# An attention and mixture-of-experts kernel: the filling of expert rows moved into the attention, and three smaller changes of order

## The reference

```
x = x + attn_a(layernorm(x))   # 16 heads, latent 32, rotary embedding, causal softmax
x = x + ffn(layernorm(x))      # 8 experts, 128 -> 512 -> 128, exact gelu; each token goes to its top 2
x = x + attn_b(layernorm(x))   # 16 heads of 8, causal softmax
x = x + ffn(layernorm(x))      # the same expert weights again
```

## Time and profile before

| what | value |
|---|---|
| median of 3 runs (1228.84 to 1236.98) | 1233.25 us |
| profiled execution: its time, its span | 1235.08 us, 1233.3 us |
| PE busy | 1038.6 us, 84% |
| DVE busy | 860.1 us, 70% |
| GpSimd busy | 734.7 us, 60% |
| ACT busy | 656.8 us, 53% |
| mean granted TensorE clock | 0.918 |
| chain that ended last | PE 50%, DVE 25%, issue 8%, SPq 7%, DMA 4%, POOL 3% |

### The profile page before, as it was taken

One profiled execution on the slowest core, in us unless ns is written; L12 is line 12 of the kernel. 1 busy time (PEld: TensorE's weight loads), 2 busy tenths in 40 slices (PEclk: granted clock), 3 DMA queues, 4 the chain that ended last, 5 costly groups with the idle time before them and its releaser, 6 DMA issues.

```text
span 1233.3 us, 31859 instructions
## 1 busy us (share of the span) xinstructions
PE 1038.6 (84%) x11223; PEld 779.5 (63%) x11224; DVE 860.1 (70%) x2217; ACT 656.8 (53%) x1205; POOL 734.7 (60%) x809
## 2 busy tenths in 40 slices
PE   4689999988888988449988888999999974499995
PEld 3466666666665656239988745666666642398995
DVE  4697889888789997525565577677777764255665
ACT  1266776656465655115544556777777741154552
POOL 0476776767667777715544424667878866155553
PEclk9699999889699999769999989999999987599998
DMA  5340000000000000222333200000000002223335
GB/s 118 82 87 3 2 2 2 11 10 10 8 10 12 11 10 19 74 55 72 96 93 92 82 18 1 2 2 10 15 17 14 19 20 70 52 76 98 101 104 147
DMA packets 69358, 53.27 MB, mean 43 GB/s; under 512 B 20770, under 2 KB 61346, under 8 KB 69218
## 3 DMA queue, kind: packets, MB, share of 16 engines
q1 hardware_dynamic: 56578, 29.78, 9.6%
q0 software_dynamic: 9088, 18.70, 4.6%
q10 hardware_dynamic: 3552, 2.95, 1.0%
HBM read 27.57 MB, written 23.81 MB: 42 GB/s over the span
## 4 chain that ended last, share of the span: by engine, by line
PE 50%; DVE 25%; issue 8%; SPq 7%; DMA 4%; POOL 3%; ACT 2%; DVEq 0%; POOLq 0%; ACTq 0%
PE PS L1851 7%; PE PS L1533 5%; PE PS L1612 5%; PE PS L1663 4%; PE PS L1535 4%; PE PS L1534 4%; PE PS L1594 3%; DMA xg<-expert_in 3%; DVE M L1004 3%; DVE swapped L1032 2%; DVE M L996 2%; PE PS L1601 2%; SPq L582 2%; PE PS L1643 2%; DVE swapped L1030 2%
## 5 line engine op out<-in xcount | busy, mean ns | idle before, releaser
L1310 ACT ACTIVATE PT<-PS 128x768 f32<-128x768 f32 x256 | 206.7, 808 | 118.0 <-PE PS L1680 69.9
L754 POOL DMA_INDIRECT expert_out<-y_rows,dest x156 | 151.9, 974 | 194.8 <-DVE y_rows L1224 170.3
L643 POOL TENSOR_SCALAR_AFFINE_SELECT PT<-PT 128x512 f32<-128x512 f32 x256 | 185.7, 726 | 85.2 <-ACT PT L1310 84.4
L1446 ACT ACTIVATE hid<-PS,b_cols 128x256 f32<-128x256 f32 x312 | 122.2, 474 | 93.9 <-PE PS L1535 93.9
L1851 PE MATMUL PS<-W,hid 128*128 x1248 | 152.3, 275 | 0.2
L660 POOL DMA_INDIRECT expert_in<-rows,slots x128 | 130.0, 1015 | 29.6 <-issue 25.0
L1851 PEld LDWEIGHTS PS<-W,hid 128*128 128x128 f32 x1248 | 146.2, 192 | 0.5 <-issue 0.5
L1612 PE MATMUL PS<-PT,v_aug 128*32 128x256 f32 (+1 forms) x2048 | 115.1, 345 | 2.5 <-POOL PT L643 2.5
L1594 PE MATMUL PS<-causal_b,ident_b 128*128 128x256 bf16 x512 | 103.8, 287 | 8.2 <-DVE q_aug L1096 7.2
L1533 PE MATMUL PS<-xg_hi,w_hi 128*128 128x256 f32 x312 | 96.4, 309 | 2.3 <-DVE xg_lo L1203 1.7
L683 POOL TENSOR_TENSOR straight<-whole,C 128x512 f32<-128x512 f32 x64 | 82.8, 1293 | 21.0 <-ACT whole L1329 19.9
(11 more groups left out here) (292 smaller groups left out, 3159.9 us busy)
## 6 DMA issues: line engine op xcount, KB each, us to landing
xg<-expert_in SPq DMA_DIRECT2D x78, 129.0 KB
got<-expert_out SPq DMA_DIRECT2D x64, 128.0 KB
expert_out<-y_rows,dest POOLq DMA_INDIRECT x156
W<-in_L_ffn_w_dram SPq DMA_DIRECT2D x1, 2048.0 KB, 10.4
expert_in<-rows,slots POOLq DMA_INDIRECT x128
expert_in<-C SPq DMA_DIRECT2D x16, 128.0 KB
out_dram<-X SPq DMA_DIRECT2D x8, 256.0 KB
b_rows<-in_L_ffn_b_dram SPq DMA_DIRECT2D x2, 512.0 KB
```

The costliest lines, as they stand in the source:

```text
L643: nc.gpsimd.affine_select(out=diagonal, in_=diagonal, pattern=[[0, 4], [1, P]], compare_op=ALU.is_ge, fill=0.0, base=0, channel_multiplier ...
L754: nc.gpsimd.indirect_dma_start(out=expert_out, out_offset=bass.IndirectOffsetOnAxis(ap=dest[:, i % 4, b_:b_ + 1], axis=0), in_=y_rows[:, i ...
L1310: s.activation(PT[:, unit % 2, 2 * pair:2 * pair + 2, 0:3 * P], PS[:, 4:6, 0:3 * P], ACT.Exp).then_inc(m["exp_done"], 1)
L1446: ins = s.activation(hid[:, r % 2, k, :], h_bank[r % 2][k // 2][:, k % 2 * ROWS:(k % 2 + 1) * ROWS], ACT.Gelu, bias=b1_cols[:, bass.ds(e * ...
```

## The change

It has four parts. `KNOWN` is chunk 4. Right after chunk 4 is ranked, DVE copies its counts to `end_of` and raises `ends_ready`; SP then fills, behind each expert's end as it stands after chunk 4, SAFE = 3 x 512 + 256 = 1792 rows, where before it filled 256 rows behind the final end. The rows come first and the single numbers second. GpSimd waits for `filled` ahead of chunk 5's sends, since these write into the filled rows. ACT's wait on `ends_ready` ahead of the experts becomes one on `attended`. SP loads the results of token tile i - 16 in slot i. In `LAST` the last output product (`out_t`, `out`) stands ahead of chunk 6's gate, and the buffers of the statistics are exchanged to suit. In attention a GpSimd's unit becomes: end the rope of the unit before, mask pair 1 of the unit before, mask pair 0, start this unit's rope, send, root.

```diff
+KNOWN = NCH - 4
+SAFE = (NCH - 1 - KNOWN) * CH + ROWS
...
-    LAST = [("rank", 0, -2, 4), ("turn", 1, 0, 7), ("gate_t", 0, -1, 0), ("gate", 0, -1, 1), ("out_t", 0, 0, 2), ("out", 0, 0, 3), ("rank", 0, -1, 4),
+    LAST = [("rank", 0, -2, 4), ("turn", 1, 0, 7), ("out_t", 0, 0, 2), ("out", 0, 0, 3), ("gate_t", 0, -1, 0), ("gate", 0, -1, 1), ("rank", 0, -1, 4),
             ("gate_t", 0, 0, 7), ("gate", 0, 0, 0), ("rank", 0, 0, 1)]
...
-                sp.wait_ge(attended[n], 1)
-                sp.dma_start(b2_rows[:, :, :].rearrange("p e d -> p (e d)"), b2.rearrange("e d -> (e d)").partition_broadcast(P)).then_inc(me["bias_ready"], 16)
-
                 sp.wait_ge(me["ends_ready"], 1)
                 with nc.allow_non_contiguous_dma(reason="one number in each row"):
                     for e in range(E):
-                        end = sp.value_load(end_of[0:1, e:e + 1], min_val=0, max_val=E * STRIDE - ROWS)
-                        sp.dma_start(expert_in[bass.ds(end, ROWS), D:WIDE].rearrange("(j p) w -> p j w", p=P),
-                                     con("aside")[:, e * RB:(e + 1) * RB].unsqueeze(2)).then_inc(me["filled"], 16)
-                        sp.dma_start(expert_in[bass.ds(end, ROWS), 0:D].rearrange("(j p) w -> p j w", p=P),
-                                     ident.unsqueeze(1).broadcast_to([P, RB, D])).then_inc(me["filled"], 16)
+                        end = sp.value_load(end_of[0:1, e:e + 1], min_val=0, max_val=E * STRIDE - SAFE)
+                        sp.dma_start(expert_in[bass.ds(end, SAFE), 0:D].rearrange("(j p) w -> p j w", p=P),
+                                     ident.unsqueeze(1).broadcast_to([P, SAFE // P, D])).then_inc(me["filled"], 16)
+                        sp.dma_start(expert_in[bass.ds(end, SAFE), D:WIDE].rearrange("(j p) w -> p j w", p=P),
+                                     con("aside")[:, e * SAFE // P:(e + 1) * SAFE // P].unsqueeze(2)).then_inc(me["filled"], 16)
+
+                sp.wait_ge(attended[n], 1)
+                sp.dma_start(b2_rows[:, :, :].rearrange("p e d -> p (e d)"), b2.rearrange("e d -> (e d)").partition_broadcast(P)).then_inc(me["bias_ready"], 16)
...
                     load(i, r, least)
-                    if least >= LAG:
-                        load_results(i - LAG, (least - LAG) % CT, least - LAG)
+                    if least > LAG:
+                        load_results(i - LAG - 1, (least - LAG - 1) % CT, least - LAG - 1)
...
                     if k == 0:
                         pool.wait_ge(m["targets_ready"], c + 1)
+                        if c == KNOWN + 1:
+
+                            pool.wait_ge(moe_sems["1" if n == "a" else "2"]["filled"], 16 * 2 * E)
...
                     if unit and plan.project[unit - 1]:
                         end_rope(plan.project[unit - 1])
+                    if unit:
+                        mask(m, unit - 1, 1)
                     mask(m, unit, 0)
+                    if plan.project[unit]:
+                        start_rope(plan.project[unit])
                     if sends_at(unit, FIRST_SENT["a"]):
                         chunk, k = sends_at(unit, FIRST_SENT["a"])
                         send("a", chunk, range(k, k + 1))
-                    if plan.project[unit]:
-                        start_rope(plan.project[unit])
-                    mask(m, unit, 1)
                     if statistics_a(unit) is not None:
                         root(m, normal_a(unit + 1)[1])
-                last_sends("a", m, 0)
+                mask(m, NCH * UNITS - 1, 1)
+                last_sends("a", m, 1)
...
+            def known_ends(m, me, s):
+
+
+                if s.c == KNOWN:
+                    dve.wait_ge(m["freed_dve"], s.freed)
+                    v.tensor_copy(end_of[:, :], counts[0:1, KNOWN, :]).then_inc(me["ends_ready"], 1)
+
```

More of the change, by code:

```diff
@@ L42 @@
 _at = 0
-for _name, _n in (("ident", P), ("cos", S), ("sin", S), ("tile_no", TILES), ("ids", 2 * CT), ("aside", (2 * E - 1) * RB), ("first_row", E), ("prefer", E), ("steps", 6), ("place", 1),
+for _name, _n in (("ident", P), ("cos", S), ("sin", S), ("tile_no", TILES), ("ids", 2 * CT), ("aside", (E * SAFE + SPARE) // P), ("first_row", E), ("prefer", E), ("steps", 6), ("place", 1),
                   ("stack", 2), ("one24", 1),
@@ L78, in constants @@
     put("ids", 2 * (p[:, None] + P * (np.arange(2 * CT) // 2)) + np.arange(2 * CT) % 2)
-    put("aside", 2 * T + p[:, None] + P * np.arange((2 * E - 1) * RB))
+    put("aside", 2 * T + p[:, None] + P * np.arange((E * SAFE + SPARE) // P))
     put("first_row", np.broadcast_to(STRIDE * np.arange(E, dtype=np.float32), (P, E)))
@@ L215 @@
     FIRST_LATE = [("key", 2, 0), ("key", 3, 0), ("prep", 0, 1), ("key", 0, 1), ("key", 1, 1), ("key", 2, 1), ("key", 3, 1), ("prep", 0, 2)]
-    LAST = [("rank", 0, -2, 4), ("turn", 1, 0, 7), ("gate_t", 0, -1, 0), ("out_t", 0, 0, 1), ("gate", 0, -1, 2), ("out", 0, 0, 3), ("rank", 0, -1, 4),
+    LAST = [("rank", 0, -2, 4), ("turn", 1, 0, 7), ("out_t", 0, 0, 1), ("out", 0, 0, 3), ("gate_t", 0, -1, 0), ("gate", 0, -1, 2), ("rank", 0, -1, 4),
             ("gate_t", 0, 0, 7), ("gate", 0, 0, 0), ("rank", 0, 0, 1)]
@@ L332, in program @@
     expert_in = nc.dram_tensor("expert_in", [E * STRIDE + SPARE, WIDE], F32, kind="Internal").ap()
-    expert_out = nc.dram_tensor("expert_out", [2 * T + E * ROWS + SPARE, D], F32, kind="Internal").ap()
+    expert_out = nc.dram_tensor("expert_out", [2 * T + E * SAFE + SPARE, D], F32, kind="Internal").ap()
     result_tiles = expert_out[0:2 * T, :].rearrange("(t p k) d -> p t (k d)", p=P, k=2)
@@ L395, in program @@
         table_i = sb("table_i", [1, 5, TILES], I32)
+        end_of = sb("end_of", [1, E], I32)
         v_aug = sb("v_aug", [P, 2, CT, H, L])
@@ L457, in program @@
             table_f = sb("table_f", [P, 5], F32, moe)
-            end_of = sb("end_of", [1, E], I32, moe)
         used = [0, 0]
@@ L558, in _ @@
             with nc.allow_non_contiguous_dma(reason="one number in each row"):
-                sp.dma_start(expert_in[E * STRIDE:, D:WIDE].rearrange("(j p) w -> p j w", p=P), con("aside")[:, E * RB:].unsqueeze(2)).then_inc(spare_filled, 16)
+                sp.dma_start(expert_in[E * STRIDE:, D:WIDE].rearrange("(j p) w -> p j w", p=P), con("aside")[:, E * SAFE // P:].unsqueeze(2)).then_inc(spare_filled, 16)
                 sp.dma_start(expert_in[E * STRIDE:, 0:D].rearrange("(j p) w -> p j w", p=P), ident.unsqueeze(1).broadcast_to([P, SPARE // P, D])).then_inc(spare_filled, 16)
@@ L615, in _ @@
                 first_late = NT - LATE
-                for tok in range(first_late, first_late + CT):
+                for tok in range(first_late - 1, first_late + CT):
                     load_results(tok, tok % CT, tok)
@@ L744, in attention_b @@
                         root(m, *root_at(unit))
-                last_sends("b", m, 1)
+                last_sends("b", m, 0)
             def send_results(n):
@@ L1017, in close @@
                         dve.wait_ge(m["freed_dve"], s.freed)
-                        statistics(m, NCH - 1, 1 if n == "b" else 0)
+                        statistics(m, NCH - 1, 0 if n == "b" else 1)
                 dve.wait_ge(m["freed_dve"], plan.find("rank", 0, NCH - 1).freed)
@@ L1063, in attention_a @@
                         closing(m, w, plan.second[unit], True)
+                        known_ends(m, moe_sems["1"], plan.second[unit])
                     if unit + 1 < NCH * UNITS:
@@ L1130, in attention_b @@
                         closing(m, w, plan.rank[unit], False)
+                        known_ends(m, moe_sems["2"], plan.rank[unit])
                     summed = statistics_at(unit)
@@ L1146, in experts @@
                 m = moe_sems[n]
-                own.did(v.tensor_copy(end_of[:, :], counts[0:1, NCH - 1, :]))
                 own.did(v.memset(begun[:, 0, :], 0.0))
@@ L1376, in attention_a @@
                     if st.kind == "gate_t":
-                        normal("a", st.c, gate_norm_b(st.c), range(2, 4) if st.c < NCH - 1 else range(CT), gate=True)
+                        normal("a", st.c, gate_norm_b(st.c), range(2, 4) if st.c < NCH - 1 else range(CT), 0 if st.c < NCH - 1 else 1, gate=True)
                     step(st)
@@ L1422, in attention_b @@
                     if st.kind == "gate_t":
-                        normal("b", st.c, gate_norm_b(st.c), range(CT), 1, gate=True)
+                        normal("b", st.c, gate_norm_b(st.c), range(CT), 1 if st.c < NCH - 1 else 0, gate=True)
                     step(st)
@@ L1427, in experts @@
                 m = moe_sems[n]
-                act.wait_ge(m["ends_ready"], 1)
+                act.wait_ge(attended["a" if n == "1" else "b"], 1)
                 s.activation(col[0][:, :], gap[:, :], ACT.Exp).then_inc(m["exp_ready"], 1)
```

1 line of the change is left out of this document (removed).

## The result

The changed kernel takes 1257.76 us (median of 4 runs, 1255.89 to 1263.01), the kernel before 1235.12 (4 runs, 1228.84 to 1250.49): ratio 1.021, interval 1.015 to 1.026. The profiled execution took 1257.98 us, its span is 1256.2, for 1235.08 and 1233.3 before; the mean granted clock is 0.918 in both. The forecast was 1205, with 1188 to 1252 as its range.

A forecast was written before the change was run, and what follows sets the result against it. The prediction saw the kernel bound by stalls between stages and DVE's and PE's waits for each other. Terms -24.7 + 10.7 - 12 - 2.3 - 2 = -30.3 against 1235.1 gave 1205 us, range 1188 to 1252.

The forecast's parts named there:

- How long do eight experts' pairs take?: Fills during the attentions: time for one expert's rows and single numbers, taken as 5.0 us, bounds 4.0 and 6.9.
- The prediction's own formula: Lateness of the fills in both attentions together: 16 times an expert's fill time less 69.3 us.
- the spare fill: Fill at the start, 1792 rows, 134 GB/s at full queues: the slow bound, 6.9 us an expert, or 9.3 by landing time.
- the small fills: Old fills behind the attentions, 79 GB/s at share 0.34: the fast bound, 232 GB/s if kept busy, 4.0 us an expert.
- the skill's rule: Writes under 512 B run as read-modify-write; 4 B numbers could cost as much as rows: 8 us an expert, 1253 us.
- Fills moved, gain side: Between attention and experts: first tile loads no longer wait for sixteen fills, 12.6 and 12.1 us earlier, -24.7 us.
- Lateness: Chunk 5's sends wait for the moved fills, late by 1.2 and 9.5 us in the two attentions: +10.7 us.
- GpSimd's order: Attention a: new instruction order keeps DVE from meeting a send with a rope product behind it: -12 us.
- the third rival: GpSimd's order gives all that chunks 4 and 5 lose, 30.7 us, as the clock stays up: 1186 us, chance 0.07.
- Last product first: End of both attentions: PE's dummy matmuls end sooner after ACT's norm, 1.5 and 0.8 us: -2.3 us.
- Results a slot later: Expert stages: SP no longer stands waiting for results not yet stored, bounds 0 and 4.6: -2 us.
- The first rival: Fill outlasts the window, running as the spare fill did: 1235, 1247 or 1253 us; slow fill's chance 0.33.

The follow-up runs named there:

- three_strides: Changed kernel with rows filled once at the start, plus three unread fills ahead, rows 512, 640 and 516 bytes apart; 1212.0 us (one run).
- rows_first: Changed kernel with all eight row fills issued ahead of the eight single-number fills; 1261.2 us, ratio 1.021.
- product_first: Kernel before with only the last output product moved ahead of chunk 6's gate and the statistics buffers swapped; 1235.0 us for 1233.5 before.
- old_fills: Changed kernel with its fills put back as before, 256 rows an expert behind the attention, and GpSimd's wait removed; 1216.5 us, ratio 0.989.
- fills_only: Kernel before with the moved fills alone; 1264.4 us, ratio 1.025.
- best_even: Changed kernel with rows filled once at the start, results loaded in the old slot, and rows 640 bytes apart; 1201.8 us, ratio 0.980.
- whole_rows: Changed kernel with rows written in pieces of 3612 bytes from a stored image, the single numbers after all rows landed; 1219.6 us, ratio 0.989.

## Why the prediction was wrong

**The step that failed is one term: "How long do eight experts' pairs take? ... I take 5.0 us".** From first issue to chunk 5's numbering, which waits for the last landing, 65.8 and 64.3 us passed; less 1.9 each for the landing, which the formula has apart, that is 7.9 an expert. The prediction's own formula, 16 times this less 69.3, gives 57 us in place of 10.7, and the sum 1251 in place of 1205; measured are 1257.8. The mechanism, the place of the wait, all that is queued behind it and the slope were as forecast. What was mis-sized is the rate, and what the runs showed in its place is that rows 516 bytes apart are slow: with rows 640 bytes apart the same fill takes 5.1 us an expert, and the kernel 1214.9 us.

It was mis-sized because of a reading of the earlier trace rows. Three rows stood there: 134 GB/s at a full queue in the spare fill, 79 at a share of 0.34 in the small fills, 291 in the stores. I weighed the small fills most, since they have "the same bytes, the same source, the same table". But their queues were a third busy, and bytes over busy share was not the rate of a full one: the start of the fill is quick in the changed kernel too (248 GB/s for 3 us), and small fills may never be more than a start; that last is not shown. And "nothing in rows of that size is slow by itself", from the stores, was true and beside the point: the stores' rows stand 512 bytes apart, the table's 516, and three_strides shows 316 GB/s for the one and 181 for the other. The one row with the same shape, target and a full queue, the spare fill, was in the text, as a bound. It gave 6.9 us because it put the single numbers at nothing beyond their bytes; rows_first has 5.5 us an expert for the rows and 2.8 for the numbers. Its other reading, 9.3 us an expert from the landing time, was over the 7.9 measured and nearer than the 5.0.

**The numbers and the skill's rule.** The sentence from the Trainium skill (DMA: Bandwidth & Descriptors, Specifications), that a write under 512 B is done as read-modify-write, gave 1253, nearest of all to the result. Its estimate was that the numbers could cost as much as the rows. Measured in rows_first: rows 44 us, numbers 22, for 14,336 pieces each. So a 4 B piece costs half of a 512 B one at 516 and nearly as much as one at an even distance (7.3 MB at 289 to 316 GB/s, 23 to 25 us). The rule's direction holds for the numbers; but what the forecast missed lay in the rows, which are not under 512 B: at an even distance, with the same 4 B writes, the fill kept the forecast's pace.

**Fills moved, gain side: -24.7.** Right in kind, too large. From chunk 7's numbering to the first load: 22.7 us before, 13.2 after, and 22.1 to 14.0: -17.6. What is late next is the table, as said, and not the last sends, but SP takes 4.2 and 3.2 us between table and load, not 2.55, and the table itself comes 9.0 and 10.8 us behind the numbering, not 7.5.

**Lateness: +10.7.** Chunk 5's numbering comes 5.9 and 6.5 us behind the last exponent before, 30.6 and 37.9 after: 24.7 and 31.4, together +56. The formula gives 57 for the measured rate. Two things that it left out cancelled: in the first attention count 4 came 4 us further ahead of the last exponent than before (40.7 us for 36.4), and the copy of the ends took 4.3 us in place of 0.16.

**GpSimd's order: -12.** Right in size: 9 and 11 us in two pairs of kernels, 13.7 on the mean at the last exponent; in the two profiled executions the last exponent is 10.3 us earlier, and chunks 4 and 5 take 18.4 us less at a clock of 0.97 for 0.85, while chunks 1 and 2 take 3.3 more:

```profile
117.20:216.40 99.20, 25.83 (x32) 1.00 0.01 2
271.20:379.40 108.20, 25.83 (x32) 0.97 0.04 12
```

The reason given is shown in part only: the collisions are fewer, and half of the edit removes them without gaining time. The clock, which only the third rival had, rose with it.

**Last product first: -2.3.** 0 and -2.6 us in the profile of product_first, and below what can be seen by medians. **Results a slot later: -2.** Wrong in sign if anything: +7 and +9 by medians in two pairs, the first clear of 1 by its ratio (1.007 to 1.016), the second not, with cause open. The waits that it was to take away stayed.

**The sum again**, with what was measured: 1235.1 - 17.6 + 56 - 11 - 2.6 = 1260, without a term for the slot; measured 1258.0. That it comes so near is luck in part: the two expert stages alone, which no term touches but the slot's, moved by -6.5 and +4.3 us, and old_fills and fills_only price the moved fills 11 us apart. The first rival had the fill's lateness, with a chance of 0.33 and prices from 1235 to 1253, without the distance of the rows as its reason; its upper price, 8.0 us an expert, is the rate that was measured.

## What to carry to other kernels

For the price of a transfer take the row that has the same shape, the same target and a full queue, though it is the worst one; here bytes over a low busy share gave 232 GB/s for what went at 119 and 131. Where rows carry a number of their own, so that they stand at a distance like 516 bytes, measure the same fill at an even distance: here it was 43 us of 1258. And fill ahead of time what does not depend on the result, so that only the part that does is left in the window: the kernel with that and without the later slot takes 1201.5 us, 0.976 of before. Even rows and the early fill do not add up (best_even): either takes away the wait.

## What the runs showed of the hardware that I had not expected

- Distance of rows: pieces of 512 bytes from SBUF went at 316, 289 and 181 GB/s with rows 512, 640 and 516 bytes apart, at a full queue each time (three_strides); pieces of 3612 bytes at 387 (whole_rows). The first thousand or so pieces at 516 are quick (248 GB/s over 3 us, 222 in rows_first).
- A copy of eight numbers by DVE took 4.30 us (436.89 to 441.19) in the first attention and 0.38 in the second. The timeline of GpSimd beside it:

```profile
436.16 1.28 POOL L665 DMA_INDIRECT expert_in<-rows,slots  x1 [0.15 <-issue]
437.47 1.29 POOL L700 TENSOR_TENSOR q_rope<-straight,swapped 128x512 f32<-128x512 f32 x1
438.70 1.22 POOL L645 TENSOR_SCALAR_AFFINE_SELECT PT<-PT 128x512 f32<-128x512 f32 x2
439.89 1.27 POOL L688 TENSOR_TENSOR straight<-whole,C 128x512 f32<-128x512 f32 x1
```

  It ended when the last of a row of GpSimd instructions did (439.89 + 1.27 = 441.16). The prediction had it at 0.16 us. It is the order of GpSimd that does it: the copy takes 4.29 or 4.30 us in attention a of all eight kernels that have both it and the new order, and 1.11 us in the two with the old order, where it ends with one GpSimd instruction (449.21 + 1.28 = 450.49 in fills_only). The timeline of DVE there:

```profile
449.39 1.11 DVE L963 CAST end_of<-counts 1x8 int32<-1x8 f32 x1
```

  The Trainium skill (SBUF — State Buffer, Who interferes with whom) counts a cast among the operations that can take the pair of ports shared with GpSimd, and says that whoever issues first holds the pair for the whole instruction while the other is blocked. These rows agree, and show the wait going on over several GpSimd instructions in a row; that the copy used those ports no row shows.
